# A fused attention and mixture-of-experts kernel: results scattered home tile by tile instead of gathered at the end

## The reference, cut to what matters

```
xn = layernorm(x)
c = xn @ w_down;  q, k, v = xn @ wq, c @ w_up;  q, k = rope(q), rope(k)
a = softmax(causal(q @ k.T * scale)) @ v @ wo
scores = sigmoid(xn @ gate_w.T);  top_scores, top_idx = top_k(scores, 2)
top_scores = 2.5 * top_scores / sum(top_scores)
routed = sum over the 2 experts of top_score * (silu(xn @ w1[e]) * (xn @ w3[e]) @ w2[e])
shared = silu(xn @ sw1) * (xn @ sw3) @ sw2
out = x + a + routed + shared
```

## Time and profile before

| | |
|---|---|
| time, median of 3 runs | 776.53 us (776.37 to 777.65) |
| the profiled execution: its own time, its span | 778.16 us, 776.4 us |
| mean granted TensorE clock | 0.976 |
| busy: PE, PEld, DVE, ACT, POOL | 92%, 83%, 83%, 76%, 64% |
| chain that ended last, by engine | PE 62%, POOL 13%, DVE 11%, issue 7%, ACT 5% |
| HBM read, written | 72.12 MB, 26.48 MB |

### The profile page before, as it was taken

One profiled execution on the slowest core, in us unless ns is written; L12 is line 12 of the kernel. 1 busy time (PEld: TensorE's weight loads), 2 busy tenths in 40 slices (PEclk: granted clock), 3 DMA queues, 4 the chain that ended last, 5 costly groups with the idle time before them and its releaser, 6 DMA issues.

```text
span 776.4 us, 15593 instructions
## 1 busy us (share of the span) xinstructions
PE 716.8 (92%) x4618; PEld 644.0 (83%) x4618; DVE 644.8 (83%) x1740; ACT 589.7 (76%) x1462; POOL 494.7 (64%) x413
## 2 busy tenths in 40 slices
PE   4899979989889999999999999999999999999944
PEld 3787768878778999999999999999999999888834
DVE  6666999878788888898888898888988888888856
ACT  3456857767768888888888888888888888888721
POOL 3443648888876567555666556665655666699862
PEclk9789999999999999999999999999999999999977
DMA  9343222443234444654545544545545443000133
GB/s 303 128 141 86 100 74 88 130 137 128 89 106 164 147 142 130 198 151 127 155 119 195 157 138 139 172 141 157 156 154 157 127 152 108 8 28 28 35 115 122
DMA packets 62066, 99.60 MB, mean 128 GB/s; under 512 B 9840, under 2 KB 34464, under 8 KB 61984
## 3 DMA queue, kind: packets, MB, share of 16 engines
q1 hardware_dynamic: 58912, 90.22, 37.8%
q0 software_dynamic: 3072, 8.39, 3.4%
HBM read 72.12 MB, written 26.48 MB: 127 GB/s over the span
## 4 chain that ended last, share of the span: by engine, by line
PE 62%; POOL 13%; DVE 11%; issue 7%; ACT 5%; another core or an unknown queue 1%; DMA 1%; SPq 0%; DVEq 0%; POOLq 0%; ACTq 0%
PE qk_proj L421 13%; PE u_acc L421 11%; PE scores L421 11%; PE ffn L421 9%; PE out_acc L421 8%; PE probs_t L532 6%; POOL swapped L902 5%; POOL xs_sorted L926 4%; POOL rot L910 3%; ACT swapped L748 2%; DVE acc L1200 2%; DVE acc L1258 2%; DVE rot L1146 1%; PE ffn L613 1%; PE ffn L587 1%
## 5 line engine op out<-in xcount | busy, mean ns | idle before, releaser
L902 POOL TENSOR_TENSOR swapped<-swapped,sin_t 128x512 f32<-128x512 f32 x128 | 164.9, 1289 | 213.2 <-DVE rot L1153 173.6
L917 POOL TENSOR_TENSOR qk_lo<-rot,qk_hi 128x512 fp32r<-128x512 f32 x128 | 163.0, 1290 | 16.8 <-ACT qk_hi L757 16.8
L1177 DVE TENSOR_TENSOR pt_lo<-probs_t,pt_hi 128x512 fp32r<-128x512 f32 x236 | 116.9, 496 | 62.2 <-ACT pt_hi L779 61.2
L768 ACT ACTIVATE probs<-scores,nbias 128x512 f32<-128x512 f32 (+3 forms) x256 | 134.9, 527 | 33.1 <-DVE nbias L1162 23.8
L748 ACT ACTIVATE swapped<-qk_proj 64x512 f32<-64x512 f32 x256 | 151.8, 593 | 7.3 <-PE qk_proj L421 2.7
L779 ACT ACTIVATE pt_hi<-probs_t 128x512 fp32r<-128x512 f32 x236 | 104.0, 441 | 46.3 <-PE probs_t L532 28.7
L1162 DVE CUSTOM_DVE_ANT_0 scores<-scores,mask 128x512 f32<-128x512 f32 (+3 forms) x256 | 125.2, 490 | 15.6 <-remote 6.9
L532 PE MATMUL probs_t<-ident,probs 128*128 128x128 f32 x600 | 105.7, 276 | 21.1 <-DVE pt_lo L1177 12.4
L1200 DVE SCALAR_TENSOR_TENSOR acc<-out_acc,rsum,acc 128x256 f32<-128x256 f32 x256 | 111.1, 475 | 2.0
L532 PEld LDWEIGHTS probs_t<-ident,probs 128*128 128x128 f32 x600 | 75.7, 141 | 36.4 <-DVE pt_lo L1177 10.0
L1146 DVE TENSOR_TENSOR rot<-qk_proj,cos_t 128x512 f32<-128x512 f32 x128 | 87.5, 683 | 12.4 <-ACT swapped L748 12.4
(11 more groups left out here) (177 smaller groups left out, 1847.9 us busy)
## 6 DMA issues: line engine op xcount, KB each, us to landing
wt<-expert_parts SPq DMA_DIRECT2D x39, 704.0 KB, 4.4
wt<-expert_parts SPq DMA_DIRECT2D x39, 512.0 KB, 4.2
raw_a<-in_attn SPq DMA_DIRECT2D x8, 768.0 KB, 5.5
xs_sorted<-u_lo SPq DMA_DIRECT2D x3, 1664.0 KB, 6.9
xs<-xs_sorted SPq DMA_DIRECT2D x39, 128.0 KB, 3.6
ys_sorted<-ysb SPq DMA_DIRECT2D x39, 128.0 KB, 4.0
expert_parts<-split SPq DMA_DIRECT2D x8, 352.0 KB, 2.3
expert_parts<-raw_f SPq DMA_DIRECT2D x8, 352.0 KB
```

The source lines that it names most:

```text
L768: ac.activation(probs[:, m % 2, PR_AT[i]:PR_AT[i] + n], s_bank[i % 2][:, 0:n], ACT.Exp, bias=nbias[:, m % 2, i:i + 1], scale=-1.0, accum_o ...
L902: pool.tensor_tensor(swapped[:, which, :], swapped[:, which, :], sin_t[:, :], ALU.mult).then_inc(sinm_ok[which], 1)
L917: pool.tensor_tensor(qk_lo[:, m % 2, which, :], rot[:, which, :], f32(qk_hi[:, m % 2, which, :]), ALU.subtract).then_inc(rlo_ok[which], 1)
L1177: ve.tensor_tensor(pt_lo[:, c], turn_bank(m, j)[:, 0:n], f32(pt_hi[:, c]), ALU.subtract).then_inc(ptlo_ok, 1)
```

## The change

- Each row of `xn` gets one more column, D, with the number of the row of its result in a new table `ys_tokens`: 1 + p + 128 t for choice 0, with 2048 more for choice 1. DVE makes the column in slot -2 (`row_ids`, three small operations); POOL adds 2048 between scatter 15 and 16, after the first 16 have landed. Rows of `xs_sorted` are so 257 elements wide; the rows that stay zero point at row 0 of `ys_tokens`, which nothing reads.
- The 32 scatters go over ten slots, 3, 3, 3, 3, 4 and again, in slots 3 to 12, and routed tiles start at slot 15 instead of 14.
- For each routed tile POOL copies the column of its rows into an index (`row_homes`, in the slot before the tile's) and scatters its 128 results by it into `ys_tokens` (`result_home`, in the slot after the tile's), in place of SP's plain store. SP's load of rows two tiles on waits for the copy.
- At the end SP reads the results back plainly, 32 loads of 128 KB in slots 56 to 59, in place of POOL's 32 gathers. The adds start at slot 58.

```diff
+DX = D + 1
-GAPS = (STILES - 3,)
+GAPS = (STILES - 3, STILES - 2)
@@ buffers and tables @@
-        xs_d = nc.dram_tensor("xs_sorted", (RTILES * P, D), F32).ap()
-        ys_d = nc.dram_tensor("ys_sorted", (RTILES * P, D), F32).ap()
+        xs_d = nc.dram_tensor("xs_sorted", (RTILES * P, DX), F32).ap()
+        ys_d = nc.dram_tensor("ys_tokens", (1 + TOP_K * TT * P, D), F32).ap()
-        xn = sb("xn", [P, TT, D])
+        xn = sb("xn", [P, TT, DX])
-        xs = sb("xs", [P, 2, D])
+        xs = sb("xs", [P, 2, DX])
+        first_id = sb("first_id", [P, 1])
+        home = sb("home", [P, 4], I32)
...
@@ the plan @@
-        def scatter_steps(s):
-            n = 4 * (s - PLACE_AT - 1)
-            return range(n, n + 4) if 0 <= n < TOP_K * TT else ()
-
-
-        GATHERS = {54: 2, 55: 2, 56: 2, 57: 2, 58: 2, 59: 2, 60: 2, 61: 7, 62: 7, 63: 4}
+
+        SCATTERS = {PLACE_AT + 1 + n: 3 + (n % 5 == 4) for n in range(10)}
+
+        def scatter_steps(s):
+            n = sum(m for at, m in SCATTERS.items() if at < s)
+            return range(n, n + SCATTERS.get(s, 0))
+
+
+        BACK = {F_LAST + 3: (0, 1), F_LAST + 4: (2, 3), F_LAST + 5: (4, 5), F_LAST + 6: (6, 7)}
-        ADDS = {(61, EARLY): 0, (61, MIDDLE): 1, (61, END): 2, (62, EARLY): 3, (62, MIDDLE): 4, (62, END): 5,
-                (63, MIDDLE): 6, (63, END): 7}
+        ADDS = {(58, EARLY): 0, (59, EARLY): 1, (60, EARLY): 2, (61, EARLY): 3, (61, MIDDLE): 4, (62, EARLY): 5,
+                (62, MIDDLE): 6, (63, MIDDLE): 7}
@@ SP @@
                 if t >= 2:
                     sp.wait_ge(fx_ok, t - 1)
+                    sp.wait_ge(home_ok, t - 1)
-            def result_out(t):
-                sp.wait_ge(yev_ok, t + 1)
-                sp.dma_start(ys_d[t * P:(t + 1) * P, :], ysb[:, t % 2, :]).then_inc(st_y[t % 2], 16)
+            def results_in(g):
+
+                if g == 0:
+                    for i in range(2):
+                        sp.wait_ge(st_y[i], 16 * len(range(i, RTILES, 2)))
+                    sp.wait_ge(m_ok, PAIRS)
+                    sp.wait_ge(y_ok, FTILES)
+                rows = [ys_d[1 + k * TT * P:][2 * g * P:2 * (g + 1) * P].rearrange("(i p) d -> i p d", p=P)
+                        for k in range(TOP_K)]
+                for i in range(2):
+                    sp.dma_start(xn[:, 2 * g + i, 0:D], rows[0][i]).then_inc(ld_rows[g], 16)
+                    sp.dma_start(back[2 * g + i], rows[1][i]).then_inc(ld_rows[g], 16)
+                for g in back_steps(s):
+                    sp.wait_ge(ulo_ok, s)
+                    results_in(g)
-                if t is not None:
-                    result_out(t)
@@ POOL @@
+                    pool.wait_ge(ids_ok, 1)
+                if n == TT:
+
+                    pool.wait_ge(st_rows, 16 * TT)
+                    pool.tensor_scalar(xn[:, :, D:DX], xn[:, :, D:DX], 1.0, float(TT * P), ALU.mult,
+                                       ALU.add).then_inc(ids2_ok, 1)
+                    pool.wait_ge(ids2_ok, 1)
-            def gather(n, head, j):
...
+            def result_home(f):
+
+                t = routed(f)
+                if t is None:
+                    return
+                pool.wait_ge(home_ok, t + 1)
+                pool.wait_ge(yev_ok, t + 1)
+
+                need(pool, st_y[(t + 1) % 2], 16 * ((t + 1) // 2))
+                pool.indirect_dma_start(out=ys_d,
+                                        out_offset=bass.IndirectOffsetOnAxis(ap=home[:, t % 4:t % 4 + 1], axis=0),
+                                        in_=ysb[:, t % 2, :], in_offset=None).then_inc(st_y[t % 2], 16)
+
+            def row_homes(f):
+                t = routed(f)
+                if t is None:
+                    return
+                pool.wait_ge(ld_xs[t % 2], 16 * (t // 2 + 1))
+                need(pool, st_y[t % 2], 16 * (t // 2 - 1))
+                pool.tensor_copy(home[:, t % 4:t % 4 + 1], xs[:, t % 2, D:DX]).then_inc(home_ok, 1)
-                for j, n in enumerate(gather_steps(s)):
-                    gather(n, s, j)
+                result_home(ffn_tile(s - 1))
+                row_homes(ffn_tile(s + 1))
@@ DVE @@
+            def row_ids():
+
+                below = route_m[:, 0:P]
+                ve.wait_ge(const_ok, 3 + 1 + 2 + 5)
+                step(ve.tensor_scalar(below, mask[:, T - P:T], -1.0, None, ALU.is_ge))
+                step(ve.tensor_reduce(first_id[:, :], below, AX.X, ALU.add))
+                ve.tensor_scalar(xn[:, :, D], steps_r[:, :, :].rearrange("p n e -> p (n e)"), first_id[:, 0:1],
+                                 None, ALU.add).then_inc(ids_ok, 1)
+                if s == LOGITS_AT - 1:
+                    row_ids()
```

More of the change, by code:

```diff
@@ L177, in moe_attention_kernel @@
         const_ok, zero_ok = sem("const_ok"), sem("zero_ok")
+        ids_ok, ids2_ok, home_ok = sem("ids_ok"), sem("ids2_ok"), sem("home_ok")
         wa_hi_ok, wa_lo_ok = sem("wa_hi_ok"), sem("wa_lo_ok")
@@ L206, in moe_attention_kernel @@
         logit_bank = out_bank[1][:, :, :].rearrange("p n d -> p (n d)")
-        zeros = u_lo[:, 0:D].bitcast(F32)
+        zeros = u_lo[:, 0:DX].bitcast(F32)
         route_t = route_m[:, 0:40 * E].rearrange("p (t e) -> p t e", e=E)
+        owner_f = route_m[:, 40 * E:40 * E + 40]
         back = [raw_f[:, n * D:n * D + D] for n in range(4)] + [raw_a[:, n * D:n * D + D] for n in range(6)] + [
@@ L273, in turn_bank, with back_steps @@
             return f_bank if late(m) and j % 2 else pt_bank
-        def gather_steps(s):
-            n = sum(m for at, m in GATHERS.items() if at < s)
-            return range(n, n + GATHERS.get(s, 0))
+        def back_steps(s):
+            return BACK.get(s, ())
         block = ctx.enter_context(nc.Block())
@@ L925, in scatter @@
                     pool.wait_ge(st_zero, 16 * 3)
+                    pool.wait_ge(ids_ok, 1)
[4 more added lines that the diff above has]
+                    pool.wait_ge(ids2_ok, 1)
                 pool.indirect_dma_start(out=xs_d, out_offset=bass.IndirectOffsetOnAxis(ap=place[:, k, t:t + 1], axis=0),
                                         in_=xn[:, t, :], in_offset=None).then_inc(st_rows, 16)
-            def gather(n, head, j):
-                t, k = divmod(n, TOP_K)
-                if n == 0:
-                    for i in range(2):
-                        pool.wait_ge(st_y[i], 16 * len(range(i, RTILES, 2)))
-                    pool.wait_ge(m_ok, PAIRS)
-                    pool.wait_ge(y_ok, FTILES)
-                if head > SLOTS - LEAD:
-                    pool.wait_ge(ptlo_ok, 4 * head + 1 + 4 * j // GATHERS[head])
-                pool.indirect_dma_start(out=xn[:, t, :] if k == 0 else back[t], out_offset=None, in_=ys_d,
-                                        in_offset=bass.IndirectOffsetOnAxis(ap=place[:, k, t:t + 1], axis=0)
-                                        ).then_inc(ld_rows[n // PER_GROUP], 16)
+            def result_home(f):
[15 more added lines that the diff above has]
+                pool.tensor_copy(home[:, t % 4:t % 4 + 1], xs[:, t % 2, D:DX]).then_inc(home_ok, 1)
             for s in range(-LEAD, SLOTS):
@@ L1137, in place_owners @@
                                       ends.unsqueeze(1).to_broadcast(all_o), ALU.is_ge))
-                step(ve.tensor_reduce(owner_f[:, :], route_t, AX.X, ALU.add))
-                ve.tensor_scalar(owner[:, :], owner_f[:, :], float(E - 1), None, ALU.min).then_inc(place_ok, 1)
+                step(ve.tensor_reduce(owner_f, route_t, AX.X, ALU.add))
+                ve.tensor_scalar(owner[:, :], owner_f, float(E - 1), None, ALU.min).then_inc(place_ok, 1)
             def cos_product(m, which):
@@ L1254, in add_routed @@
                         t = 2 * g + i
-                        of = xn[:, t, :] if k == 0 else back[t]
+                        of = xn[:, t, 0:D] if k == 0 else back[t]
                         if k == 1:
```

9 lines of the change are left out of this document (4 added, 5 removed).

## The result

The changed kernel takes 765.72 us (median of 4 runs, 764.66 to 766.73), the kernel before beside it on the same chip 777.09 us (776.37 to 779.43). The two medians are 11.4 us apart; the ratio on record is 0.984, with a 95% interval of 0.982 to 0.986, which is 11.1 to 14.2 us less. The forecast was 764.1 us, in a range of 759.5 to 773.5, and 12.4 us less. The profiled run has an own time of 764.81 us and a span of 763.0, which is 13.4 less than the 776.4 of before.

A forecast was written before the change was run, and what follows sets the result against it. POOL bounds slots 3 to 10, PE the 39 routed slots, a PE, DVE, ACT, POOL loop the late ones. -5.6 + 0.2 + 1.2 - 1.3 - 6.9 = -12.4 us off 776.5 gives 764.1, range 759.5 to 773.5.

The forecast's parts named there:

- Scatter slots, -5.6: Slots 3 to 12, set by POOL: three scatters instead of four give 11.2 us slots, a gain of 5.6 us.
- The 0.5 us for renumbering the ids in slot 8: Slot 8: POOL's small operation that renumbers the ids and two waits were priced at 0.5 us.
- The second gap: Routed tiles starting at slot 15 instead of 14: one more slot without a tile, expected to cost nothing.
- The ids, +0.2: Slot -2: three small DVE steps for the ids column, priced at 0.75 us, mostly covered, cost 0.2 us.
- The 2.5 us of cover: Slot -2: time from x_low's end to PE taking up its latents, said to cover the ids' DVE steps.
- Routed slots, +1.2: 39 routed slots: POOL's extra work hides in idle time, except 0.25 us in five slots with weights_low; 1.2 us slower.
- The rival that an indirect DMA holds PE back by itself: 39 routed slots: each added indirect DMA costs PE 0.6 us, 23.4 in all, giving 787.5 us; chance 0.10.
- The tail's adds, -1.3: Slots 58 to 63: three groups of adds moved early cost +3.9, their removal from slot ends gives -5.2; together -1.3 us.
- The hole, -6.9: Slot 62: DVE's unnamed 6.90 us wait, blamed on back-to-back POOL gathers holding back PE's completions, disappears; -6.9 us.
- the first rival: Slot 62: the hole has another cause and stays, so only 5.5 us are gained, giving 771.0 us; chance 0.33.
- More than forecast, by a full clock in the tail: Tail: without the hole PE keeps its full clock, some 3 us more could go, 759 us or less; chance 0.05.

The follow-up runs named there:

- e1: Kernel before with only the scatters over ten slots and the second gap; 772.07 us against 779.51, ratio 0.990.
- e2: Kernel before with nine of the last eighteen gathers left out, adds and stores kept; 770.94 us against 779.51, ratio 0.989.
- e11: Kernel before, unchanged, profiled again on a fourth chip; 770.73 us, and 769.90 for the same kernel beside it.
- e9: Changed kernel with the 32 scatters moved to slots 3 to 13 as 4, six times 3, 2, 3, 3, 2; 761.73 us, ratio to before 0.989.
- e6: Changed kernel with its adds at the kernel before's places in slots 61 to 63, results still loaded plainly; 765.66 us, ratio to before 0.983.
- e3: Changed kernel with twelve indirect loads put back on POOL, seven in slot 61, five in 62; 771.82 us, ratio to before 0.992.
- e7: Changed kernel with twelve indirect loads on POOL, four in each of slots 61 to 63; 765.64 us against 778.54 for before, ratio 0.982.
- e5: Changed kernel with the first three groups of adds spread over slots 57 to 60, partly behind the third row maximum; 769.92 us, ratio to before 0.988.
- e10: e9 with the first four of eight groups of adds done by POOL instead of DVE; 760.37 us, ratio to before 0.987.
- e4: Changed kernel with twelve plain loads on POOL, same size, buffers and waits as the indirect ones of e3; 765.54 us, ratio to before 0.982.
- e8: Changed kernel with the spread adds of e5 and the scatters moved to slots 3 to 13; 765.49 us, ratio to before 0.983.

## Why the prediction was right, point by point

- **Scatter slots, -5.6.** Measured -5.9: -7.2 from head 3 to 19 and +1.4 at the end of the routed tiles. Three scatters give slots of 11.0 to 11.35, four 12.61 and 12.27, slot 10 12.78, slot 3 13.06. The 0.5 us for renumbering the ids in slot 8 weren't paid: it takes 11.03, and 11.01 in e1, which has no ids. Up to 0.8 us of the gain may be the half clock in slot 11 of the kernel before (slots 11 and 12 take 21.9 us together, 21.0 in e2, which lacks that stretch), so the scatters are worth 5.1 to 5.9. The second gap, taken at nothing, is in that sum and costs nothing that can be told apart from it.
- **The ids, +0.2.** This term was too small: they cost 1.0 to 1.3 us. DVE in order of time, the rotation ahead of them and the row maximum behind them, kernel before, then changed:

```profile
55.36 0.69 DVE L1146 TENSOR_TENSOR rot<-qk_proj,cos_t 128x512 f32<-128x512 f32 x1 [2.39 <-ACT swapped L748]
...
57.19 0.29 DVE L1162 CUSTOM_DVE_ANT_0 scores<-scores,mask 128x128 f32<-128x128 f32 x1
```

```profile
54.13 0.69 DVE L1186 TENSOR_TENSOR rot<-qk_proj,cos_t 128x512 f32<-128x512 f32 x1 [1.84 <-ACT swapped L766]
54.74 0.79 DVE L1083 TENSOR_SCALAR ysb<-mask 128x128 f32<-128x128 f32 x1
...
57.23 0.29 DVE L1202 CUSTOM_DVE_ANT_0 scores<-scores,mask 128x128 f32<-128x128 f32 x1
```

  The three steps take 1.3 us and not 0.75. The changed kernel's profile reaches them 1.23 us earlier (PE's clock is 1.00 from 50 to 54 us, where before has 0.50 to 0.66) and leaves them level, which hides their price. It shows in all profiles: from POOL's sine product for the queries of head 2 to that for the keys of head 2 it is 5.64 to 5.66 us in the ten kernels with the column and 4.36 to 4.60 in the four without. The 2.5 us of cover were those of PE's latents; DVE works without a pause from the rotation ahead of the ids to the one behind, for which POOL waits, and nothing covers that. The rest of the start's 1.6 us is chance: the same start code gives 70.7, 71.7, 73.1 and 73.3 in the four profiles of kernels without the column, and 71.4 to 74.9 with it. PE is at half its clock for most of 66 to 70 us in the changed kernel's profile and at full clock in that of before, with the same work at hand (busy time by stretch, before, then changed):

```profile
66.00:68.00 2.00, 2.00 (x15) 1.70 (x13) 0.92 (x3) 0.90 (x2) 0.42 (x1) 1.00 0.00 0
68.00:70.00 2.00, 1.53 (x15) 1.33 (x12) 0.56 (x1) 1.72 (x3) 0.87 (x1) 1.00 0.00 0
```

```profile
66.00:68.00 2.00, 2.00 (x9) 1.71 (x9) 0.92 (x3) 0.90 (x2) 0.01 (x1) 0.51 0.00 0
68.00:70.00 2.00, 2.00 (x10) 1.61 (x9) 0.00 (x0) 0.12 (x1) 1.27 (x1) 0.64 0.00 0
```

- **Routed slots, +1.2.** This step failed, by sign: -1.0. The cost per slot was right (1.03 and 0.20 us on POOL, idle time 2.04 left of 3.43), but the price in the five slots with weights_low isn't paid: POOL in the changed kernel has no idle time left there, and yet the slots are as long as before, since PE sets them (10.56 us in slot 18, 10.57 before). POOL in order of time in slot 18:

```profile
293.51 1.85 POOL L901 TENSOR_TENSOR wa_lo<-raw_a,wa_hi 128x768 fp32r<-128x768 f32 x1
295.51 1.03 POOL L963 DMA_INDIRECT ys_tokens<-ysb,home  x1
296.54 0.20 POOL L973 CAST home<-xs 128x1 int32<-128x1 f32 x1
296.76 1.29 POOL L920 TENSOR_TENSOR swapped<-swapped,sin_t 128x512 f32<-128x512 f32 x1
```

  Instead each routed slot is 0.03 us shorter, in every kernel with the new way home and in none without (372.8 and 373.8). Why stays open.
- **The rival that an indirect DMA holds PE back by itself** is out: 39 of them, and a routed slot is no longer.
- **The tail's adds, -1.3.** The early groups cost 1.3 each, as said (+3.9 for three). Three groups in the tail are worth 4.7 and not 5.2, so -0.8.
- **The hole, -6.9.** The tail fell by 10.8, or 12.1 without the third early group; less 4.7 for three groups that leaves 7.4. e2 and e11 give 6.8 and 7.0 for the hole. The cause that was argued, a row of gathers without a pause, is now shown; by what path it acts is not. It has a limit that nobody could read from one profile: it needs a chip on which the hole appears. Where it doesn't, the first rival's arithmetic holds without its cause: the kernel before starts from 771, and the change is worth the rest. By the terms above, and by e9 with its 2.8 us given back against 770.97, that is some 5.5 to 6.5 us, an estimate. That the comparison was made on a chip with the hole was luck.
- **More than forecast, by a full clock in the tail.** This rival read the 0.54 of the kernel before as the hole's doing. The row doesn't show that: e6 has its adds where the kernel before has them and no hole, and PE's granted clock is 0.53 from 741.60 to 752.00 us all the same, and in the kernel before it was at 0.50 from 743 to 745 us already, ahead of the hole. The 3 us didn't come: the hole's term is 0.5 us above the wait of 6.9.
- **Sum.** -5.9 + 1.3 - 1.0 - 0.8 - 7.4 + 0.3 for the clock in the start = -13.5, against -13.4 in the spans. The errors of the terms (measured less forecast: -0.3, +1.1 for the ids, -2.2, +0.5, -0.5, and +0.3 us for the clock) cancel to -1.1; the 12.4 of the forecast owes something to that.

On the rule that speaks against the theory, the Trainium skill, SBUF — State Buffer, section "SBUF: two separate sides": it says that engine and DMA ports don't slow each other, and the change of the hole with e2, e3 and e7 shows an effect of DMA issue on compute all the same. Since by the records PE's work goes on in its place and only its news is late, no run here contradicts the rule about ports.

## What to carry to other kernels

Spread indirect DMAs, in the queue as well as in time: they cost 1.26 us each where their engine sets the pace and nothing where it idles (but look at the loads that wait for them: e9 paid 1.0 us there), and never make a long row of them without a pause beside work whose ends are waited for. Idle time of DVE or POOL is of use to an operation with its inputs in SBUF only where the other of the two stands still at that moment (e5, e10). Compare a small cost between two events close to either side of it, in several profiles: from the start of the program the ids' 1.3 us were lost in 2.6 us of chance. Before a wait with an unnamed source is explained, profile the same kernel on a second chip.

## What the runs showed of the hardware that was not expected

- A row of 128-row indirect loads without a pause delayed the news of PE's finished work by 5.3 to 6.9 us once some seven or eight of them had gone out (e3 and before: the row began at 734.1 and 735.2, the late results were finished at 743.9 and 745.2). Seven, a gap of 0.73 us and one more before a pause of 2.4 (e2), four at a time (e7) and plain loads of the same size with pauses (e4) did nothing, and on another chip twenty without a pause did nothing either (e11).
- The three profiles with a hole are from chips where the kernel before takes 777 to 780 us; the one with the row and no hole is from a chip where it takes 770. The chips of e5 to e8 (778.5) and of e9 and e10 (771) are known by the medians of the kernel before alone.
- A DVE add with both inputs in SBUF took 1.41 us instead of 0.48 beside a POOL subtraction.
- The first 70 us of one and the same code differ by 2.6 us between executions (3.5 with the ids column), with PE's granted clock at 0.5 in different stretches.
